# Transposing the layernorm output on the PE instead of by DMA through DRAM, in a fused attention and mixture-of-experts layer

## The reference, cut to what matters

```python
xn = _layernorm(x, axis=-1)                      # x: 16 x 2048 x 1024, fp16
s = attention(xn, qw, kw, vw, ow)                # 16 heads of 64, rope, causal
# mixture of experts on the same xn, 8 experts, top 2
gate_logits = xt @ Wg.T                          # xt: xn as rows of 1024
vals, sel = top_k(gate_logits, 2)
w = softmax(vals)
y = einsum('td,eod->teo', xt, We) + be           # We: 8 x 1024 x 1024, fp32
out = einsum('tk,tko->to', w, y_sel)
x = x + s * silu(out)
```

## Time and profile before

| | us |
|---|---|
| median of the runs shown | 3096.35 |
| lowest and highest of them | 3093.53, 3129.17 |
| the profiled execution | 3089.78 |
| its span on core 6, the slowest | 3088.2 |
| spans of the eight cores | 3074.3 to 3088.2 |
| busy PE, PEld | 2143.9, 791.1 |
| busy DVE, ACT, POOL | 1045.3, 941.1, 539.1 |

### The profile page before, as it was taken

One profiled execution on the slowest core, in us unless ns is written; L12 is line 12 of the kernel. 1 busy time (PEld: TensorE's weight loads), 2 busy tenths in 40 slices (PEclk: granted clock), 3 DMA queues, 4 the chain that ended last, 5 costly groups with the idle time before them and its releaser, 6 DMA issues.

```text
span 3088.2 us, 29289 instructions; the slowest of 8 cores (3074.3 to 3088.2 us)
## 1 busy us (share of the span) xinstructions
PE 2143.9 (69%) x9720; PEld 791.1 (26%) x9720; DVE 1045.3 (34%) x1432; ACT 941.1 (30%) x1245; POOL 539.1 (17%) x575
## 2 busy tenths in 40 slices
PE   0002098888499779959978991577778717777787
PEld 0002033333144334424433440111121201121212
DVE  3722156666344324414433440223121203121212
ACT  3610022222100110020010001555758604657584
POOL 0100068888300000000000000211111102211111
PEclk9999999999699889979988995588888856788888
DMA  4379823322543165164325607121010070220100
GB/s 141 127 156 110 102 73 110 109 103 103 125 83 55 33 104 83 27 122 70 55 47 92 105 3 197 23 69 61 8 55 1 1 187 6 69 68 1 55 1 28
DMA packets 418114, 229.07 MB, mean 74 GB/s; under 512 B 376480, under 2 KB 376480, under 8 KB 417456
## 3 DMA queue, kind: packets, MB, share of 16 engines
q1 hardware_dynamic: 403184, 159.54, 24.5%
q0 software_dynamic: 14784, 67.66, 9.7%
HBM read 92.67 MB, written 75.76 MB: 55 GB/s over the span
## 4 chain that ended last, share of the span: by engine, by line
PE 44%; ACT 13%; DVE 10%; SPq 9%; issue 7%; DMA 5%; POOLq 5%; POOL 5%; ACTq 0%; DVEq 0%
PE PA L634 15%; PE PB L634 14%; ACT AR L818 8%; SPq L238 8%; PE PV L737 6%; POOLq L92 5%; POOL AR L829 5%; PE PA L863 4%; DMA AR<-c_sin 3%; PE PA L808 2%; PE PB L808 2%; DVE AR L530 2%; DVE AR L536 2%; ACT AR L747 2%; DVE AR L528 2%
## 5 line engine op out<-in xcount | busy, mean ns | idle before, releaser
L634 PE MATMUL PA<-AR 128*128 128x512 f16 x2048 | 472.1, 384 | 23.4 <-DMA AR<-we 23.4
L737 PE MATMUL PV<-AR 128*128 128x512 f16 (+6 forms) x1280 | 420.7, 420 | 67.1 <-POOL AR L829 67.0
L634 PE MATMUL PB<-AR 128*128 128x512 f16 x2048 | 462.9, 379 | 0.0
L818 ACT ACTIVATE AR<-PA 128x1024 f16<-128x1024 f32 x320 | 302.9, 947 | 246.1 <-PE PA L808 244.2
L808 PE MATMUL PA<-AR 64*128 64x512 f16 x640 | 149.4, 458 | 293.1 <-ACT AR L818 142.2
L644 DVE SCALAR_TENSOR_TENSOR AR<-PA,wm,AR 128x512 f32<-128x512 f32 x256 | 192.1, 750 | 425.7 <-PE PA L634 222.9
L829 POOL TENSOR_TENSOR AR<-AR,tri 128x256 f16<-128x256 f16 x256 | 170.9, 667 | 821.0 <-ACT AR L818 796.9
L818 ACT ACTIVATE AR<-PB 128x1024 f16<-128x1024 f32 (+1 forms) x320 | 276.0, 862 | 92.6 <-PE PB L808 92.3
L644 DVE SCALAR_TENSOR_TENSOR AR<-PB,wm,AR 128x512 f32<-128x512 f32 x256 | 192.1, 750 | 249.3 <-PE PB L634 233.0
L634 PEld LDWEIGHTS PA<-AR 128*128 128x128 f16 x2048 | 202.5, 99 | 272.9 <-issue 37.5
L779 DVE TENSOR_TENSOR AR<-AR,PC 64x512 f16<-64x512 f32 x64 | 43.5, 679 | 663.2 <-PE PC L773 662.5
(11 more groups left out here) (95 smaller groups left out, 1821.7 us busy)
## 6 DMA issues: line engine op xcount, KB each, us to landing
we<-we POOLq DMA_DIRECT2D x8, 2048.0 KB, 89.6
out_c<-AR SPq DMA_DIRECT2D x8, 2048.0 KB, 8.8
v_sp<-AR POOLq DMA_DIRECT2D x32, 264.0 KB, 3.2
AR<-v_sp POOLq DMA_DIRECT2D x2, 4224.0 KB, 25.3
AR<-x_c POOLq DMA_DIRECT2D x32, 256.0 KB, 2.9
xn_sp<-AR SPq DMA_DIRECT2D x32, 256.0 KB, 2.0
AR<-c_cos SPq DMA_DIRECT2D x32, 256.0 KB, 2.7
AR<-c_sin SPq DMA_DIRECT2D x32, 256.0 KB, 3.0
```

The lines of the kernel that those rows point to most:

```text
L634: sl=slots[ib], half=half: e.matmul(PG[:, 512 * ib:512 * ib + 512], lhs, sl[:, c * D + half * 512: c * D + (half + 1) * 512], start=(c == ...
L737: nkc=nkc, p2=p2, mw=mw: e.matmul(PV2[0:mw, 512 * p2 + w0:512 * p2 + 512], v_sb[:, kc * VF + h * VW:kc * VF + h * VW + mw], expb3[sbk][:, ...
L818: W("scalar", lambda e, PS=PS, sbk=sbk, ev=ev: e.activation(ev(expb3[sbk]), ev(PS), AF.Exp, scale=1.0 / 32.0), waits=[("eT", C["eT"]), ("e ...
```

## The change

The stores to `xn_sp` and the DMA transposes are gone. A sixth layernorm step, `ln_s6`, runs one round behind `ln_s5`: for each of the eight chunks of a tile the PE transposes the 128 x 128 block of `xn16` into one of two fp16 PSUM buffers (in the banks `PC6` and `PC7`, by turns), and the block is copied into `xnT`, chunks 0, 1, 4 and 5 by the DVE and 2, 3, 6 and 7 by ACT. A transpose waits until the buffer's last reader is through. `xn16` is free for the next tile when the PE has read it, not when a store has landed. The loop over t has one round more. The gate matmuls wait for the last copies of both engines, and the first DMA of the weight cast has no wait any more.

```diff
--- before.py
+++ after.py
@@ -340,17 +340,40 @@
               waits=[("eA", tok[("sqrtd", q)]), ("eV", C["eV"])], inc="eV")
             W("vector", lambda e, q=q: e.tensor_copy(xn16[q][:, :],
                                                      xc32[q][:, :]),
-              waits=[("eV", C["eV"]), (SSP[q], 16 * (t // 4))], inc="eV")
+              waits=[("eV", C["eV"]), ("eT", tok.get(("xnrd", q), 0))],
+              inc="eV")
             tok[("mrd", q)] = C["eV"]
             W("vector", lambda e, q=q: e.tensor_scalar(
                 xn16[q][:, :], xn16[q][:, :], rc32[q][:, :], None,
                 op0=ALU.mult),
               waits=[("eV", C["eV"])], inc="eV")
             tok[("xc16", q)] = C["eV"]
-            dma("sync", xn_sp[t * 128:(t + 1) * 128, :], xn16[q][:, :],
-                SSP[q], waits=[("eV", C["eV"])])
-
-        for t in range(NT + 4):
+
+        tp16 = [PC6.bitcast(F16)[:, 0:128], PC7.bitcast(F16)[:, 0:128]]
+
+        def ln_s6(t):
+            q = t % 4
+            for c in range(NCH):
+                bp = c % 2
+                W("tensor", lambda e, q=q, c=c, bp=bp: e.transpose(
+                    tp16[bp][:, :], xn16[q][:, c * 128:(c + 1) * 128],
+                    idn[:, :]),
+                  waits=[("eV", tok[("xc16", q)]), ("scst", cst),
+                         ("eV", tok.get(("tpev", bp), 0)),
+                         ("eA", tok.get(("tpea", bp), 0))], inc="eT")
+                eng = "vector" if c % 4 < 2 else "scalar"
+                def ef(e, q=q, c=c, bp=bp, t=t):
+                    dst = xnT[:, c * T + t * 128:c * T + (t + 1) * 128]
+                    if hasattr(e, "activation"):
+                        return e.copy(dst, tp16[bp][:, :])
+                    return e.tensor_copy(dst, tp16[bp][:, :])
+                W(eng, ef, waits=[("eT", C["eT"])],
+                  inc="eV" if eng == "vector" else "eA")
+                tok[("tpev" if eng == "vector" else "tpea", bp)] = \
+                    C["eV" if eng == "vector" else "eA"]
+            tok[("xnrd", q)] = C["eT"]
+
+        for t in range(NT + 5):
             if t < NT:
                 ln_s1(t)
             if 1 <= t < NT + 1:
@@ -359,19 +382,15 @@
                 ln_s3(t - 2)
             if 3 <= t < NT + 3:
                 ln_s4(t - 3)
-            if t >= 4:
+            if 4 <= t < NT + 4:
                 ln_s5(t - 4)
-
-        spall = [("sspA", C["sspA"]), ("sspB", C["sspB"]),
-                 ("sspC", C["sspC"]), ("sspD", C["sspD"])]
-        for c in range(NCH):
-            dma("sync", c16(AR1, c * 8192, 4096)[:, :],
-                xn_sp[:, c * 128:(c + 1) * 128], "sxnT", transpose=True,
-                waits=spall)
-        xnT_rd = C["sxnT"]
-
-        dma("gpsimd", we16[0, :, :], we_h[0, :, :], "swe",
-            waits=[("sxnT", xnT_rd)])
+            if t >= 5:
+                ln_s6(t - 5)
+
+        xnT_evV, xnT_evA = C["eV"], C["eA"]
+        xnT_rd = 0
+
+        dma("gpsimd", we16[0, :, :], we_h[0, :, :], "swe")
         for ei in range(1, NE):
             dma("gpsimd", we16[ei, :, :], we_h[ei, :, :], "swe")
         dma("gpsimd", be16s[0:8, :], be_h[:, :], "sbe")
@@ -386,7 +405,8 @@
                           wgT[:, c * 24 + s3 * 8:c * 24 + s3 * 8 + 8],
                           start=(c == 0 and s3 == 0),
                           stop=(c == NCH - 1 and s3 == 2)),
-                      waits=[("sxnT", xnT_rd), ("eA", wgT_done)], inc="eT")
+                      waits=[("eV", xnT_evV), ("eA", max(wgT_done, xnT_evA))],
+                      inc="eT")
         d3 = lambda a: a.rearrange("q (t e) -> q t e", e=8)
         bc = lambda a: a.unsqueeze(2).broadcast_to([128, NT, 8])
         W("vector", lambda e: e.tensor_copy(lgall[:, :], PC6[:, 0:256]),
```

## The result

The changed kernel takes 3062.74 us (median of 9 runs), the kernel before 3093.87 beside it (10 runs); the ratio is 0.9902, 95% interval 0.9891 to 0.9914. That is 27 to 34 us faster, about 1%. I had forecast the same direction, the same mechanism and 14.5 us of gain: half of what came.

A forecast was written before the change was run, and what follows sets the result against it. The expert-weight cast was taken to bound the barrier before the projections: 71 us possible shift, less 23 x 2.42 = 55.7 and 0.8 lag, left 14.5 gain; 3089.78 - 14.5 = 3075.3, plus 3.7 gave 3079 us, range 3050 to 3106.

The forecast's parts named there:

- What bounds the stretch: Ahead of the projections' barrier: POOL's expert-weight cast sets its opening, 156.5 us after POOL may start it; router has 57.9 slack.
- The path of the gain: Cast follows tile 31's x load, delayed by 23 tiles' added time: starts 212.2 instead of 226.67; router ends 12.8 before barrier.
- the added time of a tile: Layernorm on the DVE: transposes and copies add 2.42 us a tile, 4.11 becoming 6.53.
- the prediction's legs: DVE's path from c0 to the next tile: copies, transposes and hand-overs between DVE, PE and ACT, summing to 2.42 us.
- The way through ACT: Bank's trip between transposes c2 and c4: 0.10 to ACT's start, ACT copy 0.26, 0.15 to the next transpose.
- rival B: Layernorm hand-overs cost more: at 3.05 us a tile the gain is gone (3093), at 3.39 the time is 3102; chance 0.20.
- the rest of the sum: Beyond the tile's price: 23 tiles ahead of tile 31's load, ACT's lag of 0.8, then cast start to barrier 156.5 us.
- the third rival: Layernorm hand-overs overlap better, down to 1.26 us a tile: 3052 to 3069 us; chance 0.09.
- D: Router becomes last, from 3.84 us a tile: barrier opens at 401, 18 us later than before, time 3112; chance 0.05.
- the 0.74 of the earlier trace: PE to DVE hand-over seen at the gate's end (277.21 to 277.95), used for the high bound, +0.57 a tile.
- E: Cast starts early but is held while the DVE runs layernorm, at most 8 us: 3079 to 3087; chance 0.04.
- the 71 us: Largest possible shift of the cast's start, 226.67 to 155.7, had layernorm kept its pace; 56 go to DVE copies and waits.

The follow-up runs named there:

- The run with the second cast: Changed kernel with the DVE's cast into xn16 made twice for each tile; ratio to the kernel before 0.9982 (0.9942 to 1.0022).
- eight banks: Changed kernel with eight PSUM buffers in eight banks instead of two, one for each chunk; ratio to the kernel before 0.9771 (0.9717 to 0.9826).
- the six early pieces: Weight cast cut into 32 pieces, six after tile 3's load; ratios to the kernel before: changed kernel 0.9857, with a bank per chunk 0.973, kernel before 0.9983.
- the last kernel: Changed kernel with a PSUM bank per chunk and the cast cut up, first piece after tile 4; 3002.85 us, ratio to the kernel before 0.9698.

## Why the prediction was right or wrong

*What bounds the stretch: right.* The barrier opened when the cast was through, 157.7 us after POOL could start it (197.63 to 355.37; I had 156.5 from the kernel before). Holding the cast back took the gain away, and delays put on the DVE came out at the barrier.

*The path of the gain: right.* The cast moved because the load of tile 31 moved, 23 tiles of added time before it; the router moved by its own count and stayed behind; the stages after the barrier kept their length to 0.2 us.

*The term that failed: the added time of a tile.* I had 2.42 us; the round above has 1.73, and the 23 rounds ahead of the cast have 1.80 on average. The single instructions of the round above, PE, DVE and ACT taken apart in the timeline:

```profile
104.22 0.22 DVE L369 COPY AR<-PC 128x128 f16<-128x128 f16 x1
```

```profile
104.58 0.26 PE L358 MATMUL PC<-idn,AR 128*128 128x128 f16 x1 [3.13 <-DVE AR L369]
104.93 0.27 ACT L368 COPY AR<-PC 128x128 f16<-128x128 f16 x1 [1.31 <-PE PC L358]
```

```profile
105.34 0.27 PE L358 MATMUL PC<-idn,AR 128*128 128x128 f16 x1 [0.37 <-ACT AR L368]
...
105.72 0.22 DVE L369 COPY AR<-PC 128x128 f16<-128x128 f16 x1 [1.15 <-PE PC L358]
```

Against the prediction's legs, by kind:

- The price of a copy: 0.22 and not 0.29, three times on the path, 0.21 less.
- Overlap: c0 starts before the scaling in front of it has ended (104.22 against 103.81 + 0.48 = 104.29), where I had put a gap of 0.10, 0.17 less; c4 and c5 together take 0.39, 0.05 less than two single copies.
- Hand-overs: DVE to PE (104.44 to 104.58) 0.14 and not 0.25, PE to DVE (105.61 to 105.72) 0.11 and not 0.17, together 0.17 less. The way through ACT was right to 0.02.
- Outside the legs: the wait of 0.17 between reciprocal and cast is 0.10 now, 0.08 less with rounding.

Together some 0.68, which is the difference of 2.42 and 1.73. Each error has the same sign. I had added every leg as an instruction's full length plus a gap, while DVE operations without a wait between them overlap here. The copy's price I had extrapolated from f32 copies, where the new ones are f16; whether the width or the type made it too high was not tried. Why the two hand-overs are shorter than those of the earlier trace rows is not shown either. The rounds account for the cast's start: 23 x (2.42 - 1.80) = 14.3 of the 14.6 us between 212.2 and 197.63. The forecast of a gain hung on this one term: as large an error the other way is rival B's 3.05, and no gain. The run with the second cast supports the rest of the sum, since a tile at 2.61 opened the barrier 1.5 us from where the sum puts it.

*The likeliest case was not it.* By its size the outcome is the third rival (C: hand-overs overlap better, 1.26 to 2.0), to which I gave 0.09 with the argument that c4 needs c2's reader whatever the banks do. That argument holds (the DVE does stand idle, 1.15 us, and eight banks took that away); what was wrong is that it says nothing of the other 1.3 us of my sum. That the idle time came out at 1.15, where I had some 1.1, is luck in part: the hand-overs are 0.17 shorter than I had them, and c1 ends 0.13 behind c0 and not 0.29.

*The rivals that did not come.* B and D (dearer hand-overs, router last) had the wrong sign of the error; between a transpose and a DVE copy the hand-over takes 0.11 and not the 0.74 of the earlier trace rows. E (the cast held while the DVE runs beside it) is worth at most 1.3 us: the cast took 157.7 instead of 156.5 with layernorm running beside its first 40 us, and with eight banks, again beside layernorm, 156.6 (166.05 to 322.68). The Trainium skill ("SBUF — State Buffer", section "Who interferes with whom") warns of such a hold; in these traces it is not to be seen at more than that.

*What I did not ask.* I took the 71 us by which the cast could move at most as a matter of the DVE alone. That a cast in one piece moves nothing as long as the stores stay, and that it need not stand in one piece, showed only in the runs.

## What to carry to other kernels

Find the transfer that the barrier waits for and ask what keeps it from starting; a change may pay by moving that start although its own stage becomes slower. Before letting a bulk transfer loose beside a stage, list the small DMAs on that stage's path and those in front of them in their own queue: here stores beside the cast landed after up to 134 us, and early pieces of it held up the start of layernorm. In a chain over two engines, take overlapping neighbours from a row in which they overlap, and a copy's price from a row of its type and width; where there is none, let the sum's lower bound say so.

## What the runs showed of the hardware that I had not expected

- With the cast in flight, four 256 KB stores from SP landed after 41.9 to 134.3 us instead of 2.0: they did not slip past the big transfer on POOL's queue. Beside the six early pieces SP was held 26.33 us over the issue of one 2 MB load, where it was 9.24.
- Two DVE copies of 128x128 out of two PSUM banks, with no wait between them, take 0.35 together where one takes 0.22.
- The gate's 768 matmuls take 26.39 us in one piece with all but idle DMA engines (share 0.06) and 51.6 beside the cast (226.35 to 277.95), where the PE stops 5 to 7 us after each 128 matmuls. In the last kernel the stops end with the cast: the DMA share is 0.79 from 198 to 233 and 0.02 from 233 to 241. What the PE waits for in them the trace does not say ("issue"), and no run tried it.

```profile
229.52 3.63 PE L412 MATMUL PC<-wgT,AR 128*128 128x8 f16 x128 [5.31 <-issue]
233.52 7.01 PE L412 MATMUL PC<-wgT,AR 128*128 128x8 f16 x216 [0.37 <-issue]
```
